# Layer 1's reciprocals, read back by half of the heads instead of by half of the partitions

## What is computed

```
x = x + L0_xattn(layernorm(x), ctx, ctx)          # 16 heads of 8
x = x + L0_ffn(layernorm(x))                      # 8 experts, chosen by affinity
x = x + L1_xattn(layernorm(x), ctx, mask)         # 16 heads of 64, and a null key
x = x + L1_ffn(layernorm(x))                      # ternary weights, 8-bit activations
```

```
sim  = einsum('bhid,bhjd->bhij', q * scale, k);  attn = softmax(sim)
out  = einsum('bhij,bhjd->bhid', attn, v)  ->  (b, n, 16 * 64) @ Wo  ->  layernorm
```

## Time and profile before

| | |
|---|---|
| median of 3 runs | 854.01 us (853.92 to 854.19) |
| the profiled execution | 855.46 us |
| its span, first to last instruction | 853.7 us |
| TensorE busy | 798.8 us |
| VectorE busy | 680.5 us |
| GpSimd busy | 482.6 us |
| ScalarE busy | 448.6 us |
| mean granted TensorE clock | 0.972 |

### The profile page before, as it was taken

One profiled execution on the slowest core, in us unless ns is written; L12 is line 12 of the kernel. 1 busy time (PEld: TensorE's weight loads), 2 busy tenths in 40 slices (PEclk: granted clock), 3 DMA queues, 4 the chain that ended last, 5 costly groups with the idle time before them and its releaser, 6 DMA issues. The chain is left out here.

```text
span 853.7 us, 29846 instructions
## 1 busy us (share of the span) xinstructions
PE 798.8 (94%) x11131; PEld 671.6 (79%) x11161; DVE 680.5 (80%) x1826; ACT 448.6 (53%) x1109; POOL 482.6 (57%) x971
## 2 busy tenths in 40 slices
PE   8999999998599997899999999999999999999983
PEld 6777777777497886788888888878888888888861
DVE  5888888876535554579998999989989998898876
ACT  4666666654255654435555455554555555545442
POOL 7767588877423324336465565664655646555343
PEclk9999999989799998999999999999999999999996
DMA  8966130002556651112113121121221211212110
GB/s 243 345 242 257 70 110 16 17 15 68 165 152 156 158 154 50 36 34 61 40 37 70 37 65 43 38 67 40 52 56 36 68 39 37 70 37 61 31 33 13
DMA packets 57666, 70.84 MB, mean 83 GB/s; under 512 B 8130, under 2 KB 34482, under 8 KB 57522
## 3 DMA queue, kind: packets, MB, share of 16 engines
q1 hardware_dynamic: 42658, 44.68, 20.4%
q10 hardware_dynamic: 12816, 20.06, 6.4%
q0 software_dynamic: 2048, 4.20, 1.6%
HBM read 44.54 MB, written 24.37 MB: 81 GB/s over the span
## 5 line engine op out<-in xcount | busy, mean ns | idle before, releaser
L2077 ACT ACTIVATE a_pT<-psum 128x512 f32<-128x512 f32 x128 | 69.5, 594 | 41.3 <-PE psum L1885 22.7
L721 DVE TENSOR_REDUCE l_mx<-psum 128x4 bf16<-128x512 f32 x128 | 81.8, 681 | 5.4 <-PE psum L404 3.9
L1555 POOL TENSOR_TENSOR f_hd<-f_hmc,a_wmean 128x1 f32<-128x1 f32 x32 | 6.8, 211 | 134.0 <-DVE f_hr L2337 133.2
L2234 DVE TENSOR_REDUCE a_mxf<-psum 128x8 f32<-128x1024 f32 x64 | 77.5, 1211 | 2.6 <-PE psum L1854 2.6
L1771 PEld LDWEIGHTS psum<-a_xT,a_Wq 128*128 128x128 f32 x512 | 65.7, 195 | 14.8 <-issue 13.9
L1783 PEld LDWEIGHTS psum<-a_cTm,a_Wk 128*128 128x128 f32 x512 | 65.9, 195 | 13.9 <-issue 13.9
L553 ACT ACTIVATE l_pT<-psum 128x512 f32<-128x512 f32 x128 | 70.5, 598 | 8.3 <-PE psum L422 8.0
L1864 PE MATMUL psum<-a_qT,a_kT 64*128 64x128 f32 x1024 | 71.8, 281 | 0.0
L1549 POOL TENSOR_SCALAR f_hq<-f_ht 128x512 bf16<-128x512 f32 x31 | 60.4, 1947 | 19.9 <-ACT f_ht L2122 19.8
L1771 PE MATMUL psum<-a_xT,a_Wq 128*128 128x128 f32 x512 | 70.9, 283 | 0.5 <-ACT a_xT L2060 0.5
L1833 PE MATMUL psum<-a_Wv,a_cTm 128*128 128x512 f32 x128 | 69.8, 631 | 0.1
(11 more groups left out here) (316 smaller groups left out, 2229.3 us busy)
## 6 DMA issues: line engine op xcount, KB each, us to landing
sorted_x<-r_zeros ACTq DMA_DIRECT2D x12, 1408.0 KB, 6.5
a_r_all<-a_r_rows SPq DMA_DIRECT2D x62, 256.0 KB
e_w<-in_E_W1b SPq DMA_DIRECT2D x39, 258.0 KB, 2.8
e_xt<-sorted_x SPq DMA_DIRECT2D x39, 64.0 KB, 2.4
sorted_y<-e_yt ACTq DMA_DIRECT2D x39, 64.0 KB, 2.7
a_cin<-in_ctx SPq DMA_DIRECT2D x32, 64.0 KB
out<-f_x SPq DMA_DIRECT2D x32, 64.0 KB
x_res<-in_x SPq DMA_DIRECT2D x1, 512.0 KB, 5.2
```

What stands on the lines that cost most here:

```text
L721: nc.vector.tensor_reduce(mx[:, s, Q4 * k:Q4 * k + Q4], maxp[k % 2].rearrange("p (h t) -> p h t", h=Q4), AX_X, ALU.max).then_inc(mx_ready, 1)
L2077: nc.scalar.activation(pT[:, 2 * half + e, :], tp[e], ACT.Exp, scale=SCALE).then_inc(exp_ready, 1)
L2234: nc.vector.tensor_reduce(mxf[:, 8 * half:8 * half + 8].rearrange("p (e h) -> p e h", e=2), psum[:, 0:2, :].rearrange("p e (h t) -> p e h ...
```

## The change

Each load now fills all 128 partitions of one half of the heads instead of 64 partitions of both halves, and each half has a semaphore of its own, so that `normalise(b, half)` waits for its own load. The source pattern of a load was 64 (no step) x 2 x 512; it is 2 x 64 (no step) x 512. SyncE waits for both semaphores ahead of the next store. To keep the number of semaphores, `ones_set` is merged into `rsem["set"]`: the two instructions that set the ones now count there, and every value that others wait for is two higher.

```diff
-    ones_set = sem("l0_ones_set")
...
-            g.wait_ge(rsem["set"], 5)
+            g.wait_ge(rsem["set"], 7)
...
-        nc.gpsimd.memset(v[:, 0, :, HD:], 1.0).then_inc(ones_set, 1)
+        nc.gpsimd.memset(v[:, 0, :, HD:], 1.0).then_inc(rsem["set"], 1)
...
-        nc.gpsimd.memset(v[:, 1:4, :, HD:], 1.0).then_inc(ones_set, 1)
+        nc.gpsimd.memset(v[:, 1:4, :, HD:], 1.0).then_inc(rsem["set"], 1)
...
-            pe.wait_ge(rsem["set"], 6)
+            pe.wait_ge(rsem["set"], 8)
...
-                act.wait_ge(ones_set, b + 1)
+                act.wait_ge(rsem["set"], b + 1)
...
-                act.wait_ge(rsem["set"], 1)
+                act.wait_ge(rsem["set"], 3)
...
-            dve.wait_ge(rsem["set"], 5)
+            dve.wait_ge(rsem["set"], 7)
...
-    r_stored, r_spread = sem("r_stored"), sem("r_spread")
+    r_stored, r_spread = sem("r_stored"), [sem(f"r_spread{half}") for half in range(2)]
...
             sp.wait_ge(inverse_seq, 2 * b + 2)
             if b >= 1:
-                sp.wait_ge(r_spread, 32 * b)
+                for half in range(2):
+                    sp.wait_ge(r_spread[half], 16 * b)
             sp.dma_start(r_rows, rT[0:P:G, :]).then_inc(r_stored, 16)
             sp.wait_ge(r_stored, 16 * (b + 1))
             if b >= 1:
                 sp.wait_ge(oT_ready, 2 * b)
-            for e in range(2):
-                rows = r_rows.rearrange("(a e i) q -> e a (i q)", a=2, e=2)[e]
-                sp.dma_start(r_all[e * HD:(e + 1) * HD, :, :], rows.partition_broadcast(HD)).then_inc(r_spread, 16)
+            for half in range(2):
+                rows = r_rows.rearrange("(a e i) q -> a e (i q)", a=2, e=2)[half]
+                sp.dma_start(r_all[:, half, :], rows.unsqueeze(1).broadcast_to([2, HD, Q4 * S])).then_inc(r_spread[half], 16)
...
-                dve.wait_ge(r_spread, 32 * (b + 1))
+                dve.wait_ge(r_spread[half], 16 * (b + 1))
```

## The result

The changed kernel takes 1,089.8 us (median of 4 runs, 1,089.4 to 1,091.1) beside 854.1 us for the kernel before on the same chip: a ratio of 1.2775, interval 1.2743 to 1.2808. That is 235.7 us more. The forecast was 1,115. One execution of a later run, the four loads with both products waiting for all, took 1,004.4 us at a granted clock of 0.743 and is left out as slow.

What follows compares the result with a forecast made beforehand. TensorE's work and an equally long latency loop (VectorE, store, loads) were taken to bound the kernel. Period 23.7 against 15.26, 31 times, adds 262 us to 854.0; less about one for shorter early rounds, 1,115 us, range 940 to 1,260.

Steps and rivals of the forecast that it cites:

- Nothing on this path is hidden: Layer 1's loop through VectorE, store and loads takes 15.14 us; anything added to the loads is paid 31 times.
- Two engines, by the outermost size: Each load's source has outermost size 2, so only two of 16 DMA engines work; chance 0.80 with loads queued.
- rival C: The two loads of a round use different pairs of engines: period 18.3 us, time 948 us; chance 0.05.
- 2.5 us fixed and 11.15 us for both loads: Loads from issue to landing: 2.5 us fixed, plus 11.15 us crossing on two engines at 23.5 GB/s each.
- The estimate by the Trainium skill's 27 GiB/s: Alternative engine rate for the loads: both take 9.0 us, giving a time near 1,050 us.
- Store to loads 1.98, second product 0.68: Period terms: 1.98 us from SyncE's store to the loads, 0.68 us for VectorE's product behind the last landing.
- The clock, 0.5 us a round out of 0 to 2.5: TensorE's granted clock falls after its pause, delaying the next reciprocal by 0.5 us a round, bounds 0 and 2.5.
- TensorE's busy share over a period: TensorE stands still 6 to 8 us a period, so is busy about 15 of 23 us, 65%.
- the 23.7: Forecast period of layer 1's loop in us: 23.2 from VectorE, store and loads, plus 0.5 for the clock.
- rival B: Pieces go to all 16 engines, so the first product starts on its own load: 849.5 us, 4.5 gained; chance 0.12.
- SyncE's later transfers have room: Context load and store queue behind the loads, land some 13 us after, and have a period or more until needed.

Runs made afterwards that it cites:

- the 62-and-2 kernel: The kernel before with each load of 64 partitions cut into 62 and 2, one semaphore kept: 1,117.1 us, ratio 1.3123.
- the kernels with 4 and 8: The changed kernel with the rows stored two or four times in DRAM, making the outermost size 4 or 8: 925.6 and 897.1 us.
- The experiment that took most of it away: The changed kernel plus 14 idle matmuls in TensorE's pause, rounds 4 to 31: 1,084.8 us, then 1,084.3 beside 1,089.7 for the change.
- the four-load kernel: The changed kernel with each half loaded by two transfers of 64 partitions, copies outermost, signal per half kept: 847.7 us, ratio 0.996.

## Why the prediction was right

The way, the place and the mechanism were right, and the time, 1,115 for 1,089.8, was high by 11% of the increase. Its steps in order:

- *Nothing on this path is hidden.* Right. What the loads take more, each round pays. The part from the second product to the next reciprocal was 6.88 us, as before, in the rounds where the clock was back within 4 us of the second product, and up to 7.72 where it took 6.5 us.
- *Two engines, by the outermost size.* Right, and the step that everything hung on. No row of before showed it. The 0.13 shows it after; the 62-and-2 kernel shows that the size alone does it, and the kernels with 4 and 8, with shares of 0.26 and 0.50, that the engines follow the size. The Trainium skill's rule (page "DMA: Bandwidth & Descriptors", section "Why a DMA increments its semaphore by 16 and not by 1") gives the number as the largest up to 16 that divides both slowest dimensions, and the shares of these runs agree with it at outermost sizes of 2, 4, 8 and 62. The Trainium skill also says there that on a hardware queue these are the lowest-numbered engines. The trace agrees as far as it can: the two loads queued one behind the other, share 0.13 and not 0.25, so rival C is out.
- *2.5 us fixed and 11.15 us for both loads.* Their sum was forecast as 13.65 us and is 13.19 on average. The parts were less well split. The pieces cross in 11.3 us from first to last, so 1.9 are fixed: 1.3 from the issue to the first piece, 0.6 from the last piece to the product. The forecast had found its 2.5 us of crossing before by adding up GB/s, which counts the bytes of the context load and the store as well; the pieces took 2.8. So it put too much into the fixed part and a little too little into the crossing, and the two errors partly cancel, which is luck. As for the rate, 24.5 GB/s an engine stands in the windows with the loads alone, and 23.1 over the whole crossing, with a slow first piece and the context load and the store in between. The estimate by the Trainium skill's 27 GiB/s (the same page, section "Specifications") gave near 1,050; the trace's own rate was nearer.
- *Store to loads 1.98, second product 0.68.* Right: 2.01 forecast with the 0.03 ahead of the store, 1.93 measured from the reciprocal's end, and 0.69.
- *The clock, 0.5 us a round out of 0 to 2.5.* The term is 0.4 by the timelines, and 0.84 in the worst round, inside the bounds. The reason given for taking 0.5, that a fall begins behind the pause, is wrong for most rounds: it begins up to 3 us ahead of the second product, inside the pause. What spares a round is that the clock is back early. That the size came out near is in part luck. TensorE's busy share over a period, forecast near 65%, was 17.38 of 23.00 us, 76%, since its work at half clock takes longer. The experiment that took most of it away gained 5 us in all, not 12, so its worth for the whole time is about a third of the forecast's 15. By the averages the period was 0.6 us under the 23.7: 0.46 by the loads, 0.1 by the clock, 0.08 by the store. The rest of the miss, some 5 us, is the earlier start of the loop in that execution.
- *The signal for each half, put at 4.5 us in rival B.* Rival B was not the outcome, but its mechanism is real: with 16 engines the signals gain 6 us over the same four loads without them, and 0.4% over the kernel before after paying for the two more loads.
- *SyncE's later transfers have room.* Right: VectorE never waits for `cin` or for a store in the trace after. The issue of the context load took 3.36 us instead of 0.58, and still all issues of the round were out at 610.16, 16 us before SyncE's next store. These two transfers have 256 pieces of 512 bytes together; 224 of them cross from 610.0 to 611.5 on the free engines, and the 32 of the two busy engines behind the loads, from 617.6 to 618.3. That is the "some 13 us after" of the forecast.

## What to carry to other kernels

When an access pattern is reordered, ask not only whether bytes and pieces are the same, but what stands outermost: a broadcast that moves from outermost to second place can take 14 of 16 DMA engines away. In a profile this shows as a low and flat DMA share (0.13 is two engines) exactly where an engine waits for that transfer; transfers with 64 outermost, two for each half and a signal for each half, keep both the engines and the earlier start. And before a transfer is touched, look at how long before its use it lands: here it was 0.2 us, so nearly every microsecond was paid 31 times.

## What the runs showed of the hardware that was not expected

The instruction that issues a transfer gets long behind a backlog on two engines. The context load behind the two loads took 3.36 us to issue in the round shown (median of all rounds 2.69) instead of 0.58. The four issues of the 62-and-2 kernel took 4.06 us together, where the four loads of 64 partitions took 2.37:

```profile
954.59 4.06 SPq L1442 DMA_DIRECT2D a_r_all<-a_r_rows  x4
```

With outermost 4 the context load's issue was short again, 0.48 us on average. That the queue of the two engines was full is the likely reason; no run tests it. In a round with more work for SyncE behind the loads this would be a second cost.

A piece of 2 KB took less time when fewer engines pulled: 89 ns on average with two engines (the change) and 90 with four, 98 with 16 in the four-load kernel and 122 with 16 in the kernel before. Whether this comes from the 8 KB that all engines read, or from how much crosses at once, was not tested.
